# Window attention on one core: TensorE's loop turned, two products interleaved, v masks on GpSimd, half of a kv selection on ScalarE

## The reference, cut to what matters

```python
xw = ...                                        # (2304 windows, 128, 4, 4)
qkv = jnp.einsum('nchw,oc->nohw', xw, qkv_w)    # 384 channels
pooled = _avg_pool5(qkv)                        # 5x5 sum / 25 inside the window
msq = jnp.concatenate([qkv, pooled], axis=1)    # 16 + 16 heads of 3 x 8 channels
q = relu(msq[..., :8]); k = relu(msq[..., 8:16]); v = msq[..., 16:]
v = jnp.pad(v, ..., constant_values=1.0)        # a ninth column of ones
kv = jnp.einsum('ngld,nglm->ngdm', k, v)        # 8 x 9 for each window and head
out = jnp.einsum('ngld,ngdm->nglm', q, kv)
out = out[..., :-1] / (out[..., -1:] + 1e-15)
y = jnp.einsum('nchw,oc->nohw', out, proj_w)    # 256 -> 128 channels
y = y * inv + (bn_beta - bn_mean * inv)         # batch norm
return x + y                                    # attention of _gn(x)
```

## Time and profile before

| what | us |
|---|---|
| median of 3 runs | 928.52 (928.47 to 930.1) |
| the profiled execution, its own time | 930.24 |
| its span | 928.3 |
| TensorE busy | 873.8 |
| DVE busy | 772.3 |
| ScalarE busy | 609.5 |
| GpSimd busy | 456.0 |

### The profile page before, as it was taken

How to read it: one execution, slowest core, us unless ns; L and a number is a source line. 1 busy time by engine, 2 the same in 40 slices (tenths; PEclk the granted TensorE clock), 3 DMA queues, 4 the chain that set the end, 5 groups by cost and what they waited for, 6 DMA issues and landing times.

```text
span 928.3 us, 65376 instructions
## 1 busy us (share of the span) xinstructions
PE 873.8 (94%) x29282; PEld 733.4 (79%) x29282; DVE 772.3 (83%) x1625; ACT 609.5 (66%) x1542; POOL 456.0 (49%) x967
## 2 busy tenths in 40 slices
PE   0689999999999999999999999999999999999997
PEld 0578888888888888888888888888888888888885
DVE  7369989998878898998878998999887878787886
ACT  0457676767676767676766667676767676767673
POOL 1545454545454545555554545454545454545550
PEclk9999999999999999999999999999999999999998
DMA  9910000000000000000000000000000000000000
GB/s 378 431 50 17 26 17 26 17 26 17 25 19 25 26 17 26 17 26 17 26 17 26 18 26 17 26 17 27 17 26 17 25 25 18 26 17 26 18 26 27
DMA packets 15893, 38.77 MB, mean 42 GB/s; under 512 B 1888, under 2 KB 14688, under 8 KB 15456
## 3 DMA queue, kind: packets, MB, share of 16 engines
q1 hardware_dynamic: 15840, 38.26, 10.6%
HBM read 19.38 MB, written 18.87 MB: 41 GB/s over the span
## 4 chain that ended last, share of the span: by engine, by line
PE 93%; issue 3%; DVE 2%; POOL 1%; DMA 0%; ACT 0%; DVEq 0%; POOLq 0%
PE ps L611 23%; PE ps L582 19%; PE ps L538 14%; PE ps L549 9%; PE ps L556 9%; PE ps L633 7%; PE ps L627 6%; PE ps L635 4%; PE ps L558 4%; DVE stats L377 1%; DMA x_all<-x 0%; POOL hs L234 0%; DVE kvc_full L446 0%; POOL xp L234 0%; ACT o_sb L325 0%
## 5 line engine op out<-in xcount | busy, mean ns | idle before, releaser
L255 POOL TENSOR_TENSOR xn<-x_all,mean_t 128x384 f32<-128x384 f32 x96 | 79.4, 827 | 393.6 <-PE ps L558 375.1
L305 ACT ACTIVATE vm_pool<-ps,cst 128x256 f32<-128x256 f32 x576 | 225.5, 543 | 0.4 <-PE ps L549 0.4
L446 DVE TENSOR_TENSOR kvc_full<-ps,cst 128x864 f32<-128x864 f32 x192 | 193.7, 1050 | 17.8 <-PE ps L582 17.6
L446 DVE TENSOR_TENSOR kvc_pool<-ps,cst 128x864 f32<-128x864 f32 x192 | 193.2, 1048 | 0.0
L305 ACT ACTIVATE vm_full<-ps,cst 128x384 f32<-128x384 f32 x384 | 192.2, 598 | 0.9 <-PE ps L538 0.9
L312 ACT ACTIVATE q_full<-ps 128x384 f32<-128x384 f32 x96 | 47.2, 491 | 208.5 <-PE ps L556 208.5
L538 PE MATMUL ps<-wkv_sb,xn 128*128 128x128 f32 x1152 | 145.5, 276 | 23.5 <-POOL xn L256 23.5
L538 PEld LDWEIGHTS ps<-wkv_sb,xn 128*128 128x128 f32 x1152 | 144.1, 193 | 23.5 <-issue 23.5
L452 DVE SCALAR_TENSOR_TENSOR x_all<-ps,shift,x_all 128x384 f32<-128x384 f32 x96 | 59.3, 618 | 93.4 <-PE ps L633 93.2
L611 PEld LDWEIGHTS ps<-kvc_full,q_full 64*32 64x32 f32 x9216 | 99.5, 105 | 26.4 <-issue 26.3
L611 PE MATMUL ps<-kvc_pool,q_pool 64*32 64x72 f32 x9216 | 115.8, 230 | 2.1 <-issue 2.1
(11 more groups left out here) (66 smaller groups left out, 1242.2 us busy)
## 6 DMA issues: line engine op xcount, KB each, us to landing
out<-x_all SPq DMA_DIRECT2D x96, 192.0 KB, 1.9
x_all<-x SPq DMA_DIRECT2D x3, 4608.0 KB, 32.1
x_all<-x SPq DMA_DIRECT2D x6, 768.0 KB, 8.1
cst<-consts SPq DMA_DIRECT2D x1, 172.0 KB, 11.0
wkv_sb<-wkv SPq DMA_DIRECT2D x1, 128.0 KB, 10.8
o_sb<-proj SPq DMA_DIRECT2D x1, 128.0 KB, 10.4
wq_sb<-wq SPq DMA_DIRECT2D x1, 64.0 KB, 10.5
bn_sb<-bn SPq DMA_DIRECT2D x1, 2.0 KB, 10.3
```

The costliest lines, as they stand in the source:

```text
L255: link(pool.tensor_tensor(xr, src, mean, ALU.subtract), 1)
L305: last = act.activation(heads[:, :, e, :, 0:D], src, ACT.Copy, scale=col(mask + e))
L446: last = dve.tensor_tensor(kvc[:, g], src.to_broadcast(shape), own, ALU.mult)
```

## The change: what it does

1. **TensorE's order.** The loop is turned: a turn now begins with the transposes and ends with the k/v convolution of strip s + 2. Full kv(0), pooled kv(0), q(0) and the convolution of strip 1 come ahead of the steps; two steps stand ahead of the loop and two behind it, 46 turns. Pooled out(s) and full kv(s + 1) become one block, two groups of eight out matmuls and then one tile of kv, three times. `kv_tile` and `out_tile` hold the two innermost loops of the old functions, unchanged, eight matmuls a call.
2. **PSUM.** Pooled k and v share bank 6, with one matmul of 256 columns a tile; full q goes to bank 7, pooled q to bank 6. `conv_q` has no wait any more.
3. **Full masks of v.** ScalarE makes one plain copy of v to SBUF (`v_full`, with ones already in the ninth column), and GpSimd makes the four masked copies from it (`tensor_scalar`, 432 elements each). The DVE operations that set the ones of `vm_full` once go.
4. **Own heads, pooled.** ScalarE writes the odd quads (four activations of 216 elements, one for each head of a quad, scaled by a column of the mask), then DVE the even quads in one operation of 864 elements; before, DVE did both in two.
5. **GpSimd's normalisation** is one `tensor_scalar` with two per-channel columns instead of two `tensor_tensor`.
6. **ScalarE's order** in a step: odd own heads, relu of pooled q, relu of k(s + 1), copy of v(s + 1), relu of q, then the image copies and the pooled k and v.
7. `y_done` starts at 0 instead of 1, and its readers count one less.

On TensorE, the place from the projection to the kv products at the loop's end, before. Names are output <- inputs: `ps` is PSUM, `kvc` the own-heads kv, `vm` the masked v.

```diff
+        v_full = sb("v_full", [TF, 4, KC])
...
-        K_P, V_P = 6, 7
-        Q_F, Q_P = 6, 7
+        KV_P = 6
+        assert TP * 2 * P == 512
+        Q_F, Q_P = 7, 6
...
-                    sp.wait_ge(y_done, t + (b * SPB + 2))
+                    sp.wait_ge(y_done, t + (b * SPB + 1))
...
-                src = x_all[:, bass.ds(s * SP, SP)].rearrange("p (r w c) -> p r w c", r=WS, c=WS)
-                mean = mean_t[:, bass.ds(s, 1)].unsqueeze(2).unsqueeze(3).to_broadcast([P, WS, NW, WS])
-                rstd = rstd_t[:, bass.ds(s, 1)].to_broadcast([P, SP])
-                link(pool.tensor_tensor(xr, src, mean, ALU.subtract), 1)
-                pool.tensor_tensor(xn[:, p], xn[:, p], rstd, ALU.mult).then_inc(xn_ready, 1)
+                src = x_all[:, s * SP:(s + 1) * SP].rearrange("p (r w c) -> p r w c", r=WS, c=WS)
+                pool.tensor_scalar(xr, src, mean_t[:, s:s + 1], rstd_t[:, s:s + 1], ALU.subtract,
+                                   ALU.mult).then_inc(xn_ready, 1)
...
+            def masked_v(s):
+
+                pool.wait_ge(v_copied, s + 1)
+                wait(pool, kv_f, s)
+                for e in range(EF):
+                    last = pool.tensor_scalar(vm_full[:, :, e].rearrange("p t i c -> p t (i c)"),
+                                              v_full[:].rearrange("p t i c -> p t (i c)"), col(C_VF + e), None,
+                                              ALU.mult)
+                last.then_inc(vm_f, 1)
+
             def step(s, b, at, phase):
+                if not is_last(s):
+                    masked_v(s + 1)
                 if s < NS - 2:
                     if (s + 2) % SPB == 0:
 
                         pool.wait_ge(dv_group, (s + 2) // SPB * GS + GS)
                     normalise_and_pool(s + 2, s % 2)
...
-                act.activation(k_pool[:].rearrange("p t c -> p (t c)"), ps[:, K_P, 0:TP * P],
+                act.activation(k_pool[:], ps[:, KV_P].rearrange("p (t c) -> p t c", t=TP)[:, :, 0:P],
                                ACT.Relu, scale=1 / 25.0).then_inc(km_p, 1)
 
...
+            def copy_v(s):
+                act.wait_ge(v_f, s + 1)
+                wait(act, vm_f, s)
+                act.activation(v_full[:].rearrange("p t i (h c) -> p t (i h) c", c=HC)[:, :, :, 0:D],
+                               ps[:, V_F, 0:TF * P].rearrange("p (t h m) -> p t h m", t=TF, m=D),
...
+            def masked_v_pooled(s):
+
+                act.wait_ge(rows_p, s + 1)
+                wait(act, kv_p, s)
+                heads = vm_pool[:].rearrange("p t e i (h c) -> p t e (i h) c", c=HC)
+                src = ps[:, KV_P].rearrange("p (t c) -> p t c", t=TP)[:, :, P:].rearrange("p t (h m) -> p t h m", m=D)
+                for e in range(EP):
+                    last = act.activation(heads[:, :, e, :, 0:D], src, ACT.Copy, scale=col(C_VP + e))
+                last.then_inc(vm_p, 1)
...
+            def own_heads_odd(s):
+
+                act.wait_ge(kv_p, s + 1)
+                wait(act, out_p, s)
+                src = ps[:, KVP:KVP + G, 0:HALF * KC].rearrange("p g (w c) -> p g w c", c=KC)
+                for h in range(4):
+                    at = slice(h * HC, (h + 1) * HC)
+                    last = act.activation(kvc_pool[:, :, :, 1, at], src[:, :, :, at], ACT.Copy,
+                                          scale=col(C_OWN + KC + h * HC))
+                last.then_inc(kvc_p_odd, 1)
...
             def step(s, b, at, phase):
-                relu_q(s)
+                own_heads_odd(s)
                 relu_q_pooled(s)
                 if not is_last(s):
                     relu_k(s + 1)
+                    copy_v(s + 1)
+                relu_q(s)
                 if not is_first(s):
                     to_image(s - 1)
                     pooled_out(s - 1)
                 if not is_last(s):
-                    masked_v(s + 1, False)
                     relu_k_pooled(s + 1)
-                    masked_v(s + 1, True)
+                    masked_v_pooled(s + 1)
...
+            def own_heads_even(s):
+
+                dve.wait_ge(kvc_p_odd, s + 1)
+                src = ps[:, KVP:KVP + G, 0:HALF * KC].rearrange("p g (w c) -> p g w c", c=KC)
+                own = col(C_OWN, KC).unsqueeze(1).unsqueeze(2).to_broadcast([P, G, HALF, KC])
+                dve.tensor_tensor(kvc_pool[:, :, :, 0], src, own, ALU.mult).then_inc(kvc_p, 1)
...
             def conv_kv_pooled(s, p):
                 pe.wait_ge(xp_ready, s + 1)
 
-                wait(pe, qm_f, s)
                 wait(pe, qm_p, s)
-                for half, bank, done in ((0, K_P, k_p), (1, V_P, v_p)):
-                    for t in range(TP):
-                        last = pe.matmul(ps[:, bank, t * P:(t + 1) * P], xp[:, p, t * P:(t + 1) * P],
-                                         wkv_sb[:, half * P:(half + 1) * P], start=True, stop=True)
-                    last.then_inc(done, 1)
+                for t in range(TP):
+                    last = pe.matmul(ps[:, KV_P, t * 2 * P:(t + 1) * 2 * P], xp[:, p, t * P:(t + 1) * P], wkv_sb[:],
+                                     start=True, stop=True)
+                last.then_inc(rows_p, 1)
 
             def conv_q(s, p):
 
-                pe.wait_ge(km_p, s + 1)
+
                 pe.matmul(ps[:, Q_F, 0:SP], wq_sb[:], xn[:, p], start=True, stop=True).then_inc(q_f, 1)
-                pe.wait_ge(vm_p, s + 1)
                 pe.matmul(ps[:, Q_P, 0:SPP], wq_sb[:],
                           xp[:, p].rearrange("p (q j) -> p q j", j=Q4)[:, :, 0:WP * PXP],
                           start=True, stop=True).then_inc(q_p, 1)
 
...
-                n = wins * KC
-                for t in range(tiles):
-                    for r in range(G):
-                        rows = slice(H64 * r, H64 * (r + 1))
-                        for i in range(4):
-                            last = pe.matmul(ps[Q4 * i:Q4 * (i + 1), bank + r, t * n:(t + 1) * n],
-                                             k[rows, t, Q4 * i:Q4 * (i + 1)], vm[rows, t, :, i, :],
-                                             start=True, stop=True)
-                last.then_inc(done, 1)
-
...
+            def kv_tile(pooled, t):
...
+            def out_tile(pooled, t, e):
...
+            def kv_products_pooled(s):
+                pe.wait_ge(vm_p, s + 1)
+
+                wait(pe, num_f, s)
+                pe.nop(nofuse=True)
+                for t in range(TP):
+                    last = kv_tile(True, t)
+                last.then_inc(kv_p, 1)
+
+            def out_products(s):
+
+
+                pe.wait_ge(qm_f, s + 1)
+                pe.wait_ge(kvc_p, s + 1)
+                pe.nop(nofuse=True)
+                for t in range(TF):
+                    for e in range(WF):
+                        last = out_tile(False, t, e)
+                last.then_inc(out_f, 1)
+
+            def out_products_pooled(s):
+                for t in range(TP):
+                    for e in range(WP):
+                        last = out_tile(True, t, e)
+                last.then_inc(out_p, 1)
+
+            def out_pooled_and_kv(s):
+
+
+                pe.wait_ge(vm_f, s + 2)
+
+                wait(pe, y_done, s)
+                pe.nop(nofuse=True)
+                groups = [(t, e) for t in range(TP) for e in range(WP)]
+                for i in range(TF):
+                    for t, e in groups[QG * i:QG * (i + 1)]:
+                        last = out_tile(True, t, e)
+                    if i == TF - 1:
+                        last.then_inc(out_p, 1)
+                    last = kv_tile(False, i)
+                last.then_inc(kv_f, 1)
...
             def transposes(s):
-                pe.wait_ge(num_f, s + 1)
-                pe.wait_ge(num_p, s + 1)
+
 
                 if not is_last(s):
                     pe.wait_ge(kvc_f, s + 2)
                 else:
-                    pe.wait_ge(y_done, s + 1)
+                    pe.wait_ge(num_p, s + 1)
+                    pe.wait_ge(y_done, s)
...
             def step(s, p):
-                kv_products(s, False)
-                kv_products(s, True)
-                conv_q(s, p)
-                if not is_last(s):
-                    conv_kv(s + 1, 1 - p)
+
                 if not is_first(s):
                     transposes(s - 1)
                 if not is_last(s):
                     conv_kv_pooled(s + 1, 1 - p)
                 if not is_first(s):
                     project(s - 1)
-                out_products(s, False)
-                out_products(s, True)
+                out_products(s)
+                if is_last(s):
+                    out_products_pooled(s)
+                else:
+                    out_pooled_and_kv(s)
+                    kv_products_pooled(s + 1)
+                    conv_q(s + 1, 1 - p)
+                if not is_last(s) and not is_last(s + 1):
+                    conv_kv(s + 2, p)
...
+            kv_products(0)
+            kv_products_pooled(0)
+            conv_q(0, 0)
+            conv_kv(1, 1)
+
```

(71 more changed lines are left out.)

69 lines of the change are left out of this document (25 added, 44 removed).

## The result

The changed kernel takes 1244.28 us (median of 4 runs, 1241.8 to 1245.78), the kernel before in the same comparison 929.31 us: ratio 1.3378, 95% interval 1.3352 to 1.3403. It is a third slower; my forecast was 923 us and my range ended at 941. The profiled span grew from 928.3 to 1242.8 us.

What follows compares the result with a forecast made beforehand. TensorE was taken to bound the kernel. A step of 9.11 instead of 9.185 us saves 7 us over 95 steps, the start adds 2: -5 from the 928.52 us median, 923 us forecast, eight-in-ten range 902 to 941.

Steps and rivals of the forecast that it cites:

- the packed step: TensorE's step in the kernel before without idle time, from one kv product to the next: 8.86 us.
- the two losses in it: Per two-step turn, 0.20 us waiting for ScalarE's last pooled mask and 0.45 us at the loop's branch.
- The branch: TensorE's loop branch, now behind the 1.34 us k/v convolution, was to cost nothing instead of 0.45 us a turn.
- R4: Rival: the loop's branch is still paid, 0.35 us idle in 46 turns, +16 us, 939 us; chance 7%.
- The masks on GpSimd: GpSimd's four full masks were taken at 0.6 us each, under the 0.79 us limit, so hidden.
- R3: Rival: GpSimd's masks exceed 0.79 us each and delay the block; at 0.9 us, 965 us; chance 9%.
- The chain through image copy, projection and residual: Late image copy delays the projection to 1.52 us, residual ends at 3.94, block starts at 4.08; step 9.11 us.
- R1: Rival: the chain is shorter than added up and TensorE stays packed, 8.80 us a step, 894 us; chance 13%.
- The interleaving: Pooled out and full kv mixed in one TensorE block take 1.68 us, against 1.86 us apart.
- R2: Rival: the interleaved block doesn't overlap and takes 1.86 us, step 9.29 us, 941 us; chance 13%.
- The start: First masks stand behind GpSimd's two first normalisations, moving the first full kv by 0 to 5 us, taken as +2.

Runs made afterwards that it cites:

- e7: Changed kernel with two full masks on ScalarE, two on GpSimd (`tensor_tensor`), pooled out and full kv apart, one step ahead of the loop: 892.02 us.
- e1: Changed kernel with GpSimd's four full masks as `tensor_tensor` with a broadcast mask column instead of `tensor_scalar`: 977.46 us.
- e8: Changed kernel with four more matmuls of 320 columns on TensorE in each step, where it waits for GpSimd's masks: 1150.94 us.
- e4: Changed kernel with only the first of GpSimd's four full masks made, the other places holding ones: 944.92 us.
- e9: e7 with the change's interleaved block of pooled out and full kv and its waits: 940.88 us.
- e10: Changed kernel with GpSimd's four `tensor_scalar` masks replaced by plain `tensor_copy` of v, without masking: 945.83 us (one run).
- e6: Changed kernel with full masks back on ScalarE, one step ahead of TensorE's loop and three behind instead of two and two: 928.68 us.

## Why the prediction was wrong

- **What bounds the kernel before, the packed step, the two losses in it**: right. With both losses gone and nothing put in their place (e7), a step takes 8.63 us; the packed sum was 8.86. The 0.23 between them weren't packed: see the interleaving below.
- **The branch**: right, no idle time at it in the changed kernel, 46 turns. From the last k/v convolution to the transposes it is 0.112 us from start to start, with the branch between them and without it, in e7 too. R4 is refuted. The Trainium skill's rule in "Runtime: NRT & Kernel Launch", section "Instruction fetch mechanics", on taken branches out of the fetched window, didn't cost a turn anything here; whether a fetch took place behind the queued work the trace doesn't tell.
- **The masks on GpSimd: the step that failed.** I bounded an operation without a row by a memset and a `tensor_tensor`, 0.4 to 0.93 us, and took 0.6 "because only one operand streams in". It takes 1.366 us. R3 had the right mechanism with 9%, and its own price (0.9 us a mask, 965 us) was what `tensor_tensor` costs: 977 us in e1. By R3's own sum a mask of 1.366 us gives 923 + 4 x (1.366 - 0.79) x 95 = 1142 us; with the clock held up, e8 took 1151. The fault was to take the costliest known operation as upper end of an unknown one.
- **The rule that I weighed there.** The Trainium skill, "GPSIMD Engine Reference", section "3.1 Elementwise — side-by-side cycle accounting", led to an estimate of 0.37 us before dispatch for one streamed input; the plain copy's 0.546 us is 0.18 above it, which dispatch may or may not explain, and `tensor_scalar`'s 1.29 to 1.37 us is more than three times it. The measurement decides.
- **What wasn't in the forecast at all: the clock.** Once TensorE idles 2.4 us in every step, its granted clock falls in about two steps of three. This made the loss 87 us larger (e8).
- **The chain through image copy, projection and residual**: right, 9.17 against 9.18 us (e4), so TensorE doesn't stay packed and R1 fails. But its price was higher than counted, since without it the base is 8.63 and not 8.86. The stalls are 0.21 and 0.32 us; I had 0.20 and 0.25, and for R1 I took half of them as 0.14, where my own terms give 0.22.
- **The interleaving**: the term of 1.68 us was mis-sized (1.75), and the upper end of 1.86 for "apart" too (1.73 in e7). I read 1.10 us for 96 out products as 11.5 ns an instruction. But the first and the last of them start 0.98 us apart before and in e7 alike. The rest stands between two groups of products. From the last full out product to the first pooled one it is 0.121 us before and 0.010 in e7 (medians of 71 and 76 steps). From pooled out to full kv it is 0.121 us where no branch stands between (0.572 with it, so the branch's 0.45 were read right), and 0.009 in e7. Before, the next group has four waits ahead of it in the first place and three in the second, in e7 one and two. R2's conclusion, no overlap, is right, by e9.
- **The start**: +2 us, measured some 12 in e4. I had counted the later masks (first q convolution at 36.73 instead of 32.68) but not the code that is written out once more, ahead of the loop and, for another 3 us, behind it.
- Had GpSimd been fast enough, the change would have been at 945 us (e4, e10), slower by 1.5% and not faster by 0.6%.

Still open: why `tensor_scalar` costs GpSimd more than twice a copy, and whether it is the number of waits that makes the extra 0.11 us between two groups of products in the kernel before; no run changes that alone.

## What to carry to other kernels

An operation without a row of its own on an engine has no upper end from other operations: time it alone before a step is hung on it, above all on GpSimd, where the same elements cost 0.55, 0.91 or 1.37 us by the operation chosen. Work moved to an idle engine must be placed by when its result is needed, and here half of it fitted and the whole did not. Before two stages of TensorE are interleaved, look at the waits of both: the block inherits the later one.

## What the runs showed of the hardware

- GpSimd, 128 x 432 float32: copy 0.546 us, `tensor_tensor` with a broadcast column 0.906, `tensor_scalar` with a constant 1.291, with a column 1.366; with two columns on 384 elements 1.651.
- More matmuls made a waiting kernel 93 us faster, by holding TensorE's clock at its upper level (e8, 1150.94 against 1244.28 us).
- TensorE's code costs 0.8 to 2.0 us of idle time at places where it is run for the first time, also long after the loads are over (e6: 1.70, 1.24 and 0.99 us at 899, 909 and 918 us).
